# A decoder layer on one core: products of the maxima spread over key tiles, all items ahead, stage transposes at the end of a tick

## The reference

```python
x = x + attn_ref(layernorm(x))             # banded scores of 64 keys, no softmax, then a layer norm
x = x + xattn_ref(layernorm(x), ctx, ctx)  # 16 heads of 16, softmax over 1601 keys
x = x + ffn_ref(layernorm(x))              # see below

def ffn_ref(src):
    ...
    scores = einsum('bqhd,bkhd->bhqk', q, k) * 16 ** -0.5
    probs = softmax(scores)                # 16 heads, 2048 keys, no mask
    x = layer_norm(src + attn @ Wo + bo)
    # each token goes through one of 4 experts, by floor(x @ router_w + router_b) mod 4
    return layer_norm(x + expert(x))
```

## Time and profile before

| | |
|---|---|
| median of three runs | 1926.76 us (1913.13 to 1932.7) |
| the profiled execution | 1925.12 us, span 1923.4 us |
| granted TensorE clock, mean | 0.904 |
| PE busy | 1635.3 us, 85% |
| VectorE (DVE) busy | 1409.4 us, 73% |
| ScalarE (ACT) busy | 1209.6 us, 63% |
| maxima: reduces L690 | x1024, 1082.2 us |
| exponentials L679 | x1856, 958.8 us |

### The profile page before, as it was taken

One profiled execution on the slowest core, in us unless ns is written; L12 is line 12 of the kernel. 1 busy time (PEld: TensorE's weight loads), 2 busy tenths in 40 slices (PEclk: granted clock), 3 DMA queues, 4 the chain that ended last, 5 costly groups with the idle time before them and its releaser, 6 DMA issues.

```text
span 1923.4 us, 28344 instructions
## 1 busy us (share of the span) xinstructions
PE 1635.3 (85%) x10301; PEld 623.0 (32%) x10301; DVE 1409.4 (73%) x1992; ACT 1209.6 (63%) x2434; POOL 136.5 (7%) x183
## 2 busy tenths in 40 slices
PE   7997688888888886966586999999999997875997
PEld 6862122222222221144311222222222221133996
DVE  5788688888888884034576999999999995035454
ACT  1173367777777776534304788888888887542654
POOL 2100000000000000021300000000000000022343
PEclk9997799999999998578857999999999999565999
DMA  6010000000000000000010000000000000051111
GB/s 148 6 30 1 1 1 1 1 1 1 1 1 1 1 1 1 1 1 0 3 42 1 1 2 1 1 1 1 1 1 1 1 1 1 0 202 39 49 50 39
DMA packets 29841, 30.60 MB, mean 16 GB/s; under 512 B 10652, under 2 KB 26590, under 8 KB 29726
## 3 DMA queue, kind: packets, MB, share of 16 engines
q1 hardware_dynamic: 26990, 21.99, 4.0%
q0 software_dynamic: 2736, 7.08, 1.2%
HBM read 22.63 MB, written 6.68 MB: 15 GB/s over the span
## 4 chain that ended last, share of the span: by engine, by line
PE 69%; DVE 20%; ACT 6%; issue 2%; SPq 2%; DMA 1%; POOL 0%; DVEq 0%; POOLq 0%; ACTq 0%
PE bank L627 23%; PE bank L618 16%; DVE nm_part L690 15%; PE s_pair L606 8%; ACT p_arena L679 5%; PE s_pair L977 4%; PE bank L995 3%; PE bank L363 3%; PE s_pair L363 2%; PE s_pair L187 2%; SPq L732 2%; PE s_pair L769 1%; PE s_pair L636 1%; PE bank L177 1%; PE bank L340 1%
## 5 line engine op out<-in xcount | busy, mean ns | idle before, releaser
L690 DVE TENSOR_REDUCE nm_part<-s_pair 128x1 f32<-128x802 f32 (+1 forms) x1024 | 1082.2, 1102 | 128.6 <-PE s_pair L606 122.1
L679 ACT ACTIVATE p_arena<-bank 128x512 f32<-128x512 f32 (+1 forms) x1856 | 958.8, 602 | 339.2 <-PE bank L618 339.1
L606 PE MATMUL s_pair<-k_op,q_arena 48*128 48x401 f16 (+1 forms) x2048 | 614.9, 377 | 74.5 <-DVE nm_part L690 67.2
L618 PE MATMUL bank<-q_arena,k_op 49*128 49x512 f16 (+1 forms) x1856 | 564.4, 399 | 91.8 <-ACT p_arena L679 48.0
L627 PE MATMUL bank<-p_arena,v_aug 128*32 128x512 f32 (+1 forms) x3712 | 525.0, 640 | 0.0
L618 PEld LDWEIGHTS bank<-q_arena,k_op 49*128 49x128 f16 (+1 forms) x1856 | 144.9, 95 | 569.3 <-ACT p_arena L679 454.2
L606 PEld LDWEIGHTS s_pair<-k_op,q_arena 48*128 48x128 f16 x2048 | 136.6, 95 | 363.8 <-DVE nm_part L690 341.5
L627 PEld LDWEIGHTS bank<-p_arena,v_aug 128*32 128x32 f32 (+1 forms) x3712 | 74.8, 110 | 129.9 <-issue 73.2
L709 DVE RECIPROCAL rden<-s_pair 128x16 f32<-128x16 f32 x32 | 8.2, 258 | 140.3 <-PE s_pair L636 139.5
L977 PE MATMUL s_pair<-q_arena 128*128 128x128 f32 x608 | 73.3, 280 | 3.4 <-ACT q_arena L1018 2.9
L977 PEld LDWEIGHTS s_pair<-q_arena 128*128 128x128 f32 x608 | 72.9, 197 | 5.0 <-issue 3.1
(11 more groups left out here) (179 smaller groups left out, 1149.9 us busy)
## 6 DMA issues: line engine op xcount, KB each, us to landing
q_arena<-nm_T SPq DMA_DIRECT2D x512, 0.2 KB
k_op<-in_L_ffn_W SPq DMA_DIRECT2D x1, 4096.0 KB, 13.0
v_aug<-in_L_ffn_W SPq DMA_DIRECT2D x1, 4096.0 KB, 24.6
res_rows<-x_sb SPq DMA_DIRECT2D x1, 2048.0 KB, 7.5
x_rows<-src_sb SPq DMA_DIRECT2D x4, 512.0 KB, 3.3
x_sb<-in_x SPq DMA_DIRECT2D x1, 1536.0 KB, 11.3
p_arena<-in_ctx SPq DMA_DIRECT2D x12, 128.0 KB, 2.0
q_arena<-in_L_attn_W_qkv SPq DMA_DIRECT2D x1, 768.0 KB, 5.5
```

Source lines behind the costliest of these rows:

```text
L606: last = pe.matmul(m_tile[slot % 2][:, part * 512:part * 512 + at.width], q_op[rows, pair, at_q:at_q + P], k_op[rows, pair, k0:k0 + at.wid ...
L618: pe.matmul(score_bank[k % 3][0:m, :], k_op[rows, pair, kt * P:kt * P + m], q_op[rows, pair, b // 4 * QG:(b // 4 + 1) * QG], start=True, s ...
L679: act.activation(prob[0:m, k % 8, :], score_bank[k % 3][0:m, :], ACT.Exp, scale=SCALE).then_inc(z["exp"], 1)
L690: dve.tensor_reduce(nm_part[:, b % 2, qt, a, c:c + 1], m_tile[slot % 2][:, :].rearrange("p (h k) -> p h k", h=2)[:, :, 0:at.width], AX.XY, ...
```

## The change

Three edits.

1. Stages: on TensorE and on ScalarE the transposes of k and q and their evictions move from the start of the tick to its end. v always goes to the first half of bank 5, so the second part of a projection now waits until VectorE has added the bias to v of the tile before ("v" semaphore).
2. Attention: all 44 items are made in front of block 0.
3. Attention: single products ("parts", two to an item) are dealt evenly to the key tiles, 64 to a block: five or four to a tile in cross, four in self. Four stand between the scores, the rest behind the sums. An item may begin in one key tile and end in the next. The result of a block is turned at the first key tile from `RESULT_AT` on behind which no item is half done.

```diff
@@ stage_tensor, tick
-                if st.has_kv and (i := tile_at(t, f + 3, n)) is not None:
...
                 if (i := tile_at(t, f + 2, n)) is not None:
...
-                        dest = bank(st.proj_banks[q])[0:m, 0:w] if at == 0 else bank(5)[0:m, q * C:q * C + w]
+                        dest = bank(st.proj_banks[q] if at == 0 else 5)[0:m, 0:w]
+                        if at and some(i):
+                            pe.wait_ge(z["v"], i)
...
                     last.then_inc(z["aT_ps"], 1)
+                if st.has_kv and (i := tile_at(t, f + 3, n)) is not None:
...
@@ stage_scalar, tick
...
@@ stage_vector, tick
-                    v_ps = bank(5)[0:m, q * C:(q + 1) * C] if first == 2 * C else bank(st.proj_banks[q])[0:m, C:2 * C]
+                    v_ps = bank(5)[0:m, 0:C] if first == 2 * C else bank(st.proj_banks[q])[0:m, C:2 * C]
...
-                                      ALU.add)
+                                      ALU.add).then_inc(z["v"], 1)
@@ Attention
+            def parts_at(self, b, kt):
+                low, high = (min(2 * (ITEMS + LEAD) + 2 * ITEMS * (self.n * b + k) // self.n, 2 * ITEMS * BLOCKS) for k in (kt, kt + 1))
+                return range(low, high)
             def items_at(self, b, kt):
-                low, high = (ITEMS * (b + 1) + (LEAD if b else 0), ITEMS * (b + 2) + LEAD)
-                low, high = min(low, ITEMS * BLOCKS), min(high, ITEMS * BLOCKS)
-                return range(low + (high - low) * kt // self.n, low + (high - low) * (kt + 1) // self.n)
+                parts = self.parts_at(b, kt)
+                return range(parts.start // 2, parts.stop // 2)
+            def result_after(self, b, kt):
+                whole = [k for k in range(RESULT_AT, self.n) if self.parts_at(b, k).stop % 2 == 0]
+                return b > 0 and kt == whole[0]
             def heads_at(self, b, kt):
-                first = self.items_at(b, kt)
-                return (1, 3, 0, 2) if first and self.item(first[0])[0] % 2 == 0 else (0, 2, 1, 3)
+                halves = [self.item(p // 2)[0] % 2 for p in self.parts_at(b, kt)][:4]
+                if sorted(halves) != [0, 0, 1, 1]:
+                    halves = [1, 1, 0, 0]
+                free = {0: [0, 2], 1: [1, 3]}
+                return tuple(free[1 - h].pop(0) for h in halves)
@@ attention_tensor
-            for n in range(ITEMS):
-                maximum(n, 0)
-                maximum(n, 1)
+            for part in range(2 * (ITEMS + LEAD)):
+                maximum(part // 2, part % 2)
             for b in range(BLOCKS):
                 for kt in range(at.n):
-                    items = at.items_at(b, kt)
-                    for half in range(2):
-                        for i in range(2):
-                            score(b, kt, 2 * half + i)
-                            if half < len(items):
-                                maximum(items[half], i)
+                    parts = at.parts_at(b, kt)
+                    for i in range(4):
+                        score(b, kt, i)
+                        if i < len(parts):
+                            maximum(parts[i] // 2, parts[i] % 2)
...
-                    for n in items[2:]:
-                        maximum(n, 0)
-                        maximum(n, 1)
-                    if kt == RESULT_AT and b:
+                    for part in parts[4:]:
+                        maximum(part // 2, part % 2)
+                    if at.result_after(b, kt):
                         turn_sums(b - 1)
@@ attention_vector
-            for n in range(ITEMS):
+            for n in range(ITEMS + LEAD):
...
```

More of the change, by code:

```diff
@@ L318, in __init__ @@
                 self.s = {n: ctx.enter_context(nc.semaphore(f"{name}_{n}")) for n in (
-                    "in0", "in1", "ln", "root", "xT_ps", "xT", "proj", "sum", "hi", "split", "copy", "kT", "kop", "qT", "qop",
+                    "in0", "in1", "ln", "root", "xT_ps", "xT", "proj", "sum", "v", "hi", "split", "copy", "kT", "kop", "qT", "qop",
                     "at", "aT_ps", "aT", "o_ps", "kept", "res", "res_bias")}
@@ L391, in tick @@
                     last.then_inc(z["aT_ps"], 1)
+                if st.has_kv and (i := tile_at(t, f + 3, n)) is not None:
+                    q, m = (r - f - 3) % 2, st.rows(i)
+                    pe.wait_ge(z["split"], i + 1)
+                    pe.wait_ge(z["copy"], i + 1)
+                    if some(i):
+                        pe.wait_ge(z["kop"], i)
+                    for pair in range(H // 2):
+                        last = pe.transpose(bank(6).bitcast(fp16)[:, pair * P:pair * P + m],
+                                            k_tok[0:m, q, 2 * pair:2 * pair + 2, :].rearrange("p h s -> p (h s)"),
+                                            ident16[0:m, 0:m])
+                    last.then_inc(z["kT"], 1)
+                if st.has_q and (i := tile_at(t, f + 3, n)) is not None:
+                    q = (r - f - 3) % 2
+                    pe.wait_ge(z["split"], i + 1)
+                    pe.wait_ge(z["copy"], i + 1)
+                    if some(i):
+                        pe.wait_ge(z["qop"], i)
+                    for pair in range(H // 2):
+                        last = pe.transpose(bank(7).bitcast(fp16)[:, pair * P:(pair + 1) * P],
+                                            q_tok[:, q, 2 * pair:2 * pair + 2, :].rearrange("p h s -> p (h s)"), ident16[:, :])
+                    last.then_inc(z["qT"], 1)
             return tick
@@ L398, in tick @@
             def tick(t, r):
[L399 to L409, removed]
                 if (i := tile_at(t, f + 1, n)) is not None:
@@ L572, in __init__ @@
                     "m_ready", "m_free", "nm", "nm_T", "q_max", "score", "exp", "pv", "o_sb", "recip")}
-                self.item_slot, self.result_slot, at = {n: n for n in range(ITEMS)}, {}, ITEMS
+                self.item_slot, self.result_slot, at = {n: n for n in range(ITEMS + LEAD)}, {}, ITEMS + LEAD
                 for b in range(BLOCKS):
```

13 lines of the change are left out of this document (12 added, 1 removed).

## The result

The changed kernel takes 1816.85 us (median of 4 runs, 1811.80 to 1818.00) where the kernel before takes 1924.2 beside it (4 runs): a ratio of 0.944, with an interval of 0.940 to 0.948. The forecast was 1839, range 1795 to 1872. The profiled execution took 1815.74 us, with a span of 1814.0; before, the span was 1923.4. So there are 109.4 us to be found between the two traces.

What follows compares the result with a forecast made beforehand. Bounds: TensorE and VectorE taking turns in the stage between attentions, TensorE's key-tile chain, and half-clock stretches after a stand. Stage -47, cross +2, self -40, post stage -1: total -86, from 1925 to 1839 us, range 1795 to 1872.

Steps and rivals of the forecast that it cites:

- Stage: Between the attentions: ticks shrink from 8.64 to 5.5 us, and the end after GpSimd's add gets 6 us shorter; -47 us.
- the ring: Stage tick between attentions: VectorE's chain 3.81 us, about 0.15 to wake TensorE, x transposes to VectorE's start 1.40; sum 5.4.
- Rival (d): Stage between attentions: the clock, not VectorE, sets ticks at 7.0 us; +20 us, total 1859; chance 0.06.
- Settled cross blocks: Cross attention: VectorE's reduce enters every key tile's chain, blocks go from 35.9 to 38.2 us; +28 us over twelve blocks.
- Rival (c): Cross attention: even spreading keeps VectorE's reduce out of the chain; 0 to -23 instead of +28, total 1788 to 1811; chance 0.13.
- Block 0: First attention blocks: items made ahead leave ordinary work plus three tiles at 1.2 GHz; self -9.5 with later start, cross -3.
- Blocks 14 and 15: Attention ends: TensorE's 10.25 us stand for bias rows goes, clock holds; cross -6 and -17, self -10.5 and -20 us.
- Rival (f): Block 15: TensorE still stands because bias rows come late; +8 and the half clock's 17, total 1864 us; chance 0.03.
- rival (b): Both attentions' tails: clock falls once items end, block 15 gains nothing; +37, total 1890 us; chance 0.12.
- rival (a): Turn to cross block 15: clock falls to 1.2 GHz and stays low; +16, total 1855 us; chance 0.22.
- Behind the self attention: Post stage after the self attention: a little earlier at 2.4 GHz, -1 us.
- Rival (e): Settled cross blocks: TensorE waits before every second sums lower the clock; costs up to 216 us, total 2055; chance 0.02.

Runs made afterwards that it cites:

- whole items: Changed kernel with the cross attention's products dealt as 4 or 6 per key tile instead of 4 or 5, all 44 items still ahead: 1793.75 us, ratio 0.939.
- idle products: Kernel with whole items plus products nobody reads beside the scores in the last three key tiles of cross block 14 and first three of 15: 1791.85 us.
- last items late: Changed kernel with the last 20 items spread over all of block 14, as in the kernel before: 1871.65 us, ratio 0.977.
- evictions first: Changed kernel with ScalarE's evictions of the k and q transposes back at the start of its tick: 1850.37 us, ratio 0.963.
- half reduce: Changed kernel with VectorE's cross-attention reduce reading only the first half of each product's keys: 1749.9 us, ratio 0.906.
- attention alone: Kernel before with only the attention edits, its stages as before: 1870.66 us, ratio 0.969.
- stage alone: Kernel before with only the stage edits, its attentions as before: 1872.18 us, ratio 0.975.

## Why the prediction was right

The sign, and the mechanism of every large term, came out; the forecast took 86 us off the profiled execution where 109.4 went, so it was a fifth too small. The largest misses in size are the settled cross blocks (6.7 us), the part behind the self attention (5.3) and cross blocks 0 and 1 (4.4); cross block 15 missed by 4.8 the other way. Part of that is luck: when the clock rises in block 0 and behind the self attention was guessed, behind the cross attention it was in no term, and it moves these by several us between executions.

*Stage.* Ticks of 5.35 us (mean of the same 13) where 5.5 was said and 8.64 was; the ring is the one that was walked, 3.82 + 0.06 + 1.47, where 0.15 had been put for waking TensorE. Evictions put back in front make it 7.0, at full clock. Rival (d), that the clock would hold the ring at 7.0, fell: the window of these ticks has a clock of 0.99. Behind the end of GpSimd's add the attention starts after 5.3 us (907.3 to 912.6), 7 were said. Stage -49.8 for -47.

*Stage before the cross attention.* Said 0, within 3; it gave 2.7. The traces with the changed stages have their first reduce at 162.3 to 165.3, the two with the old ones at 165.8 and 166.5, so some 2 us may be the order's, and the rest is spread. Another 2.4 us went between the last cross score and the first L453. It goes with the clock: every trace whose cross block 15 ended at the half clock has 12.1 us there, every other one 9.7 to 10.0.

*Settled cross blocks.* The pair of tiles was said at 5.79 and is 5.74. The block was said at 38.2 and is 37.66, and that is mostly the turned result. The prediction took its 0.9 us before as what was left over from its walk, and added 0.2. Read off the tiles, the two around the result take 6.06 us before where a pair takes 5.43, and 6.36 after for 5.74: 0.63 and 0.62, so the result costs no more than it did, and the walk of the block before was some 0.3 us short. Twelve blocks make +21.3 for +28. Rival (c), spreading without a chain, was refuted by the changed trace, and by both sides of the experiment: whole items take the wait out of every second tile (-25 us with all that follows from it), a reduce of half the length takes nearly all of it out (-4.3 us a block).

*Block 0.* Cross was given three slow tiles. It had one and part of another (3.94 and 3.38 where 2.59 and 3.05 are usual), the first, with no sums in it, took 1.93, and the clock rose 7.0 us after the first score instead of 12.3. With block 1 the term is -8.4 for -4. That is luck in part: in the other traces with these products block 0 took 37.5 to 40.7 us, 39.15 in the repeat of the changed kernel. Self had two slow tiles (3.15 and 4.3) and part of a third; -14.0 for -12.5 (the later start of 2.9 us was said at 3).

*Blocks 14 and 15.* The stand went, as said; -6.9 and -10.8 for -6 and -10.5. Rival (f) fell: of the waits for bias rows 1.0 us is left. Self block 15 held 2.4 GHz to the end, -20.0 for -20, so rival (b) fell. Cross block 15 is the term between forecast and rival (a): the clock did fall at the turn that (a) named, in the second tile of the block (772.4, where the block starts at 768.28), behind the sums over 65 keys, but came back after 10.2 us, and the block was 34.5 us to its last score; the -12.2 are for -17 of the forecast and about -1 of the rival. "Entered so, block 15 stays low as before" was its wrong step, in this execution: three other kernels with this turn stayed low to the end in their profiled executions. The fall itself costs 4 us here, as idle products show.

*Behind the self attention.* Said -1, measured -6.3. The two windows have the same work; the first went from 64.3 to 59.5 us at a clock of 0.65 for 0.59, the second from 155.4 to 154.0. TensorE was busy 4.6 us less in the first and 1.0 in the second for the same work, so it is the clock. But the gain can't be put down to the change: the part took 219.7 to 231.3 us in the traces behind the changed attention and its variants, and in the one that entered it at the half clock (last items late) 220.4. What sets the clock's return there stays open: with the same work it was low for 44 us in one kernel and for 72 in the next.

*Rival (e)* didn't come: the settled cross blocks have a clock of 1.00 despite a wait in each tile.

## What to carry to other kernels

When two engines hand tiles to each other through two buffers, walk the chain of one tile with the traced times, product by product, before changing how work is spread: an even count that completes an item in the middle put a latency of 1.44 us (0.39 from a product to the reduce, 0.93 the reduce, 0.12 to the next product) into every tile where it had been in every second one, and cost 21 us although no engine was full. Move the last piece of work that a transfer waits for to an earlier place, rather than spreading it to the last moment; here this gave 50 us, 32 of it through the clock that the stand had dropped. In a ring of engines, put in front what the other engine waits for next, and judge the order by the ring's length, not by an engine's busy time.

## What the hardware showed that was not expected

The same key tiles run at either clock, depending on how they are entered. Self block 15 of the changed kernel has no items and holds 2.4 GHz in tiles of 2.39 us for its 38 us; that of the kernel before, entered after a stand, stays at 0.50 for 58.4 us in tiles of 3.69. "TensorE: Matmul & The Clock Gate" in the Trainium skill (part 1) says that activity releases the throttle; the block that holds its clock agrees with this, and the block that never gets it back, with scores and sums in every tile, does not.

The turn to cross block 15, with sums over 65 keys and no items, is an unstable place. In the changed kernel and with whole items the clock fell there and came back after some 10 us (four profiled executions, two of each); in the traces of evictions first, half reduce and attention alone it fell and stayed low to the block's end; with unread products beside the scores it didn't fall (three). The traces show one difference: in the four the fall came 4.1 to 4.5 us after the block's first score, and the clock was back 0.1 to 0.9 us behind the tile that also turns a result (4.74 us); in the three the fall came 3.3 to 3.8 us after it. Whether that decides the return, no run shows. The same turn in blocks with items cost some 1.2 us in a few blocks: of the kernel before and the stage alone, of the kernels with whole items (37.0 to 37.2 instead of 35.86 us), and, of those with single products, of half reduce and last items late; it did in no block of the changed kernel's two traces.

Beside GpSimd's add over all of x, 8.99 us after, a cast on VectorE that otherwise takes 0.29 us still takes 5.73, and ends 0.15 us behind the add. Timeline of the end of the stage after (before: the earlier trace rows):

```profile
898.31 8.99 POOL L934 TENSOR_TENSOR x_sb<-x_sb,rows 128x4096 f32<-128x4096 f32 x1
...
901.72 5.73 DVE L476 CAST q_tok<-p_arena 128x256 f16<-128x256 f32 x1
```

The adds of biases that read a bank ran on VectorE in the same 9 us at their usual length (L448, 0.69 us, and L457, 0.41); the stalled one is the cast. No run took GpSimd's add away, so that it is the cause is read from the ends alone.
